# Attention with masks on VectorE, copied first keys and queries, and two heads in the halves of the rows; another order of the down products

## The reference

```python
# attention (x normalized first; B=8, S=512, D=256, 16 heads of 16)
scores = einsum('bhqd,bhkd->bhqk', Q, K) * 16 ** -0.5
scores = scores + where((abs(i - j) <= 64) | (i == 0) | (j == 0), 0, -inf)
x = x + (softmax(scores) @ V) @ Wo + bo
# experts: 16, each takes its 512 best of 4096 rows
topk_weight, topk_idx = top_k(softmax(flat_x @ gate_w.T, -1).T, 512)
g, u = xg @ Wg[e].T, xg @ Wu[e].T                # width 1024
eo = (gelu(g) * u) @ Wd[e].T * topk_weight       # the down product
out = scatter_add(eo) + shared_expert(x)
```

## Time and profile before

| | |
|---|---|
| median of three runs | 1411.79 us |
| the profiled execution, its own time | 1400.23 us |
| its span, first to last instruction | 1398.5 us |
| busy in the span: PE, PEld, DVE, ACT, POOL | 90%, 76%, 61%, 43%, 42% |
| mean granted TensorE clock | 0.952 of full |
| `qs<-qk_parts`, `ks<-qk_parts` | 96 transfers each, 128 KB |
| `qs<-mt` | 128 transfers, 4 KB |
| `rd<-rden` | 16 transfers, 256 KB |

### The profile page before, as it was taken

How to read it: one execution, slowest core, us unless ns; L and a number is a source line. 1 busy time by engine, 2 the same in 40 slices (tenths; PEclk the granted TensorE clock), 3 DMA queues, 4 the chain that set the end, 5 groups by cost and what they waited for, 6 DMA issues and landing times. The chain is left out here.

```text
span 1398.5 us, 26404 instructions
## 1 busy us (share of the span) xinstructions
PE 1256.7 (90%) x9930; PEld 1066.7 (76%) x9930; DVE 849.4 (61%) x1510; ACT 597.1 (43%) x1023; POOL 584.9 (42%) x530
## 2 busy tenths in 40 slices
PE   2995999999999972699999599999999999999997
PEld 2884777777777752588887578888888888888886
DVE  7874555555555512695688676666666666666641
ACT  1340544444444442354222255455455454545442
POOL 6000333332333342462200146666666666665554
PEclk9996999999999985699999789999999999999999
DMA  2778555555555416441003144434444433344411
GB/s 84 262 249 136 79 88 90 86 86 92 93 93 93 71 50 198 144 149 57 15 31 121 51 161 121 115 105 113 120 121 121 121 111 105 109 114 121 121 31 15
DMA packets 71284, 148.44 MB, mean 106 GB/s; under 512 B 14736, under 2 KB 31520, under 8 KB 64928
## 3 DMA queue, kind: packets, MB, share of 16 engines
q1 hardware_dynamic: 58544, 128.39, 35.4%
q0 software_dynamic: 12656, 18.90, 7.4%
HBM read 104.53 MB, written 42.21 MB: 105 GB/s over the span
## 5 line engine op out<-in xcount | busy, mean ns | idle before, releaser
L610 ACT ACTIVATE pt<-ps_p 128x512 f32<-128x512 f32 (+1 forms) x320 | 170.0, 582 | 218.1 <-PE ps_x L673 122.7
L550 DVE TENSOR_REDUCE mx<-ps_s 128x2 f32<-128x384 f32 (+2 forms) x160 | 143.9, 900 | 171.9 <-PE ps_x L651 154.9
L1803 POOL TENSOR_TENSOR h_lo<-h,h_hi 128x512 fp32r<-128x512 f32 x128 | 175.5, 1383 | 136.1 <-ACT h_hi L1839 135.8
L454 POOL TENSOR_SCALAR_AFFINE_SELECT pt<-pt 128x512 f32<-128x512 f32 x192 | 110.1, 597 | 273.4 <-ACT pt L610 273.4
L1913 PE MATMUL ps_gu<-xt_hi,w_hi 128*128 128x512 f32 x512 | 203.5, 397 | 2.1 <-DVE xt_lo L1862 2.1
L1913 PE MATMUL ps_gu<-xt_lo,w_hi 128*128 128x512 f32 x512 | 200.8, 392 | 0.0
L1913 PE MATMUL ps_gu<-xt_hi,w_lo 128*128 128x512 f32 x512 | 200.3, 391 | 0.0
L1878 DVE TENSOR_TENSOR h<-ge,ps_gu 128x512 f32<-128x512 f32 x128 | 87.8, 686 | 180.1 <-ACT ge L1833 167.9
L1740 DVE TENSOR_TENSOR w_lo<-w,w_hi 128x768 fp32r<-128x768 f32 x128 | 173.5, 1360 | 31.3 <-ACT w_hi L1735 27.8
L648 PE MATMUL ps_s<-ks,qs 96*128 96x256 f32 (+2 forms) x512 | 171.6, 398 | 0.0
L1812 POOL DMA_INDIRECT out<-ys,idx x64 | 131.1, 2049 | 73.3 <-ACT ys L1849 61.8
(11 more groups left out here) (221 smaller groups left out, 2891.9 us busy)
## 6 DMA issues: line engine op xcount, KB each, us to landing
w<-in_We SPq DMA_DIRECT2D x48, 1024.0 KB, 4.9
qk_parts<-qk SPq DMA_DIRECT2D x8, 2048.0 KB, 7.7
qs<-qk_parts SPq DMA_DIRECT2D x96, 128.0 KB, 3.6
ks<-qk_parts SPq DMA_DIRECT2D x96, 128.0 KB, 5.0
x<-in_x SPq DMA_DIRECT2D x16, 512.0 KB, 8.7
attn_t<-on SPq DMA_DIRECT2D x32, 256.0 KB, 3.7
ot<-attn_t SPq DMA_DIRECT2D x32, 128.0 KB
rd<-rden SPq DMA_DIRECT2D x16, 256.0 KB
```

Source lines behind the costliest of these rows:

```text
L454: last = pool.affine_select(out=part, in_=part, pattern=[[0, HQ], [sign, hi - lo]], compare_op=ALU.is_ge, fill=0.0, base=0, channel_multip ...
L550: last = dve.tensor_reduce(mxu[:, h:h + n, j], tile[:, :, 0:N0 if j == 0 else W[j]], AX, ALU.max)
L610: act.activation(pt[i][:, t % 2, h:h + nh], ps_p[:, n % 2].rearrange("p (h q) -> p h q", h=nh)[:, :, 0:W[i]], ACT.Exp, scale=SCALE).then_i ...
L1803: pool.tensor_tensor(h_lo[:, m], h32[:, (e * KI + m) % HB], h_hi[:, m].bitcast(F32), ALU.subtract).then_inc(hlo_s, 1)
```

## The change

Attention. The scratch tensor, `qs` and `ks` get rows of 516 (`ZS`): behind each tile of 128 stands a copy of column 0, which GpSimd makes in `project` before the store. A band of keys or queries then takes two more columns (`WZ`: 258, 258, 194) and contains key 0 or query 0 once or twice, so the two-column products, the separate maximum and the separate exponentials of query 0 are gone. The four heads of a unit stand two by two in the halves of the partitions: heads 0 and 2 in rows 0 to 49, heads 1 and 3 in rows 64 to 113. A product has 48 or 64 rows where it had 96 or 128. The loads become 12 per unit, the copies of the maxima 12 (two halves of four blocks and two single columns). The mask products of the maxima are gone: one VectorE instruction per head and tile (16 per unit) adds the mask to the scores and takes the maximum. `ps_s` becomes a ring of three banks, each with one head and tile. ScalarE does 8 exponentials per unit, each of two heads, where it did 10. GpSimd's selects are cut into pieces of 64 columns, 11 per unit. All loops over units are unrolled. SP's order per unit stays.

Experts. Row tiles 0 and 1 of the down product first take k tiles 0 to 6, then k tile 7 each; row tiles 2 and 3 follow as before.

```diff
-M_ROW = 96
+M_ROW = 48
+RING = 3
+ZC = P + 1
+ZS = NT * ZC
+WZ = [w + 2 for w in W]
+SIDE = ZC + 1
...
-        ks = att.enter_context(nc.sbuf_tensor("ks", [P, UB, HQ, S], F32R))
-        qs = att.enter_context(nc.sbuf_tensor("qs", [P, UB, HQ, S], F32R))
+        ks = att.enter_context(nc.sbuf_tensor("ks", [P, UB, HQ // 2, ZS], F32R))
+        qs = att.enter_context(nc.sbuf_tensor("qs", [P, UB, HQ // 2, ZS], F32R))
...
+                for b in range(B):
+                    pool.wait_ge(qlo_s, b * 4 + 4)
+                    rows = qk[:, b % 2].rearrange("p c m k i -> p (c m) k i")
+                    pool.tensor_copy(rows[:, :, :, P], rows[:, :, 0, 0:1].to_broadcast([P, 4 * KD, NT])).then_inc(z_s, 1)
...
-        ps_s = ctx.enter_context(nc.psum_tensor("ps_s", [P, 2, 2 * S], F32))
-        ps_p = ctx.enter_context(nc.psum_tensor("ps_p", [P, 2, S], F32))
-        ps_x = ctx.enter_context(nc.psum_tensor("ps_x", [P, 2, HQ, NT - 1, 2], F32))
-        key0, query0 = ps_x[:, 0], ps_x[:, 1]
+        ps_s = ctx.enter_context(nc.psum_tensor("ps_s", [P, RING, S], F32))
+        ps_p = ctx.enter_context(nc.psum_tensor("ps_p", [P, 2, 2, S], F32))
...
+                def near_only(u, i):
+                    pool.wait_ge(exp_s, u * SJ + 2 * (i + 1))
+                    for n in range(W[i] // WIN):
+                        first, sign = (n * (WIN + 1), 1) if n < 2 else (UPPER[i] + (n - 2) * (WIN + 1), -1)
+                        part = pt[i][:, u % 2, :, first:first + WIN]
+                        last = pool.affine_select(out=part, in_=part, pattern=[[0, HQ], [sign, WIN]], compare_op=ALU.is_ge,
+                                                  fill=0.0, base=sign * (n % 2) * WIN, channel_multiplier=-sign)
...
+                def load(u):
+                    b, t = u // UB, u % UB
+                    for dst, parts in ((qs, (0, 0, 1)), (ks, (2, 3, 2))):
+                        for n, part in enumerate(parts):
+                            heads = d["qk"][b, part, t * HQ * DH:(t + 1) * HQ * DH, :].rearrange(
+                                "(p r c) q -> r c p q", r=2, c=DH)
+                            for r in range(2):
+                                row = 64 * r + DH * n
+                                sp.dma_start(dst[row:row + DH, t].bitcast(F32), heads[r]).then_inc(qk_in[t], 16)
+
+                def m_rows(u):
+                    t = u % UB
+                    sp.wait_ge(mt_s, u + 1)
+                    for r in range(2):
+                        rows = qs[64 * r + M_ROW:64 * r + M_ROW + 2, t].bitcast(F32)
+                        for k in range(MK):
+                            dst = rows.rearrange("c p (j i) -> c (p j) i", j=NT)[:, :, 32 * k:32 * k + 32]
+                            sp.dma_start(dst, mt[32 * k + 16 * r:32 * k + 16 * r + 16, u % 2]).then_inc(m_in[t], 16)
+                        for z in (1, 2):
+                            sp.dma_start(rows[:, :, ZC * z + P:ZC * (z + 1)], mt[16 * r:16 * r + 16:NT, u % 2, 0:1],
+                                         allow_slow_non_contiguous=True).then_inc(m_in[t], 16)
...
+                m_rows(0)
+                for u in range(NU):
+                    b, t = u // UB, u % UB
+                    if u + 1 < NU:
+                        m_rows(u + 1)
+                    if u + UB < NU:
+                        sp.wait_ge(st_s, (u + 1) * SJ)
+                        load(u + UB)
+                    if u >= 1:
+                        store(u - 1)
...
+                    for g, (j, h) in enumerate(SCORES):
+                        dve.wait_ge(sc_s, u * SG + g + 1)
+                        n, m = (S, mask[:, 0:S]) if j == 0 else (WZ[j], mask[:, S:S + WZ[j]])
+                        dve.tensor_tensor_reduce(junk[:, (u * SG + g) % RING, 0:n], ps_s[:, (u * SG + g) % RING, 0:n], m, 1.0, -3e38, ALU.add, ALU.max,
+                                                 mx[:, u % 2, h % 2, h // 2, j:j + 1]).then_inc(mx_s, 1)
...
+                    if n >= RING:
+                        pe.wait_ge(mx_s, n + 1 - RING)
+                    rows = slice(64 * (h % 2), 64 * (h % 2) + M_ROW)
+                    q = tile_of(qs[rows, t, h // 2], j)
+                    k = ks[rows, t, h // 2]
+                    k = whole(k) if j == 0 else window(k, j)
+                    out = ps_s[:, n % RING]
+                    out = out.rearrange("p (k c) -> p k c", c=P) if j == 0 else out[:, 0:WZ[j]]
+                    pe.matmul(out, q, k, start=True, stop=True).then_inc(sc_s, 1)
...
+                AV = {3: 0, 5: 1, 6: 2, 7: 3}
+                for u in range(NU):
+                    for n in range(SJ):
+                        if u + 2 < NU:
+                            score(u + 2, 2 * n)
+                            score(u + 2, 2 * n + 1)
+                        exponents(u, n)
+                        if u >= 1 and n in AV:
+                            times_v(u - 1, AV[n])
...
+                    if e > 0:
+                        pe.wait_ge(ys_s, e * CT)
+                    contract(0, range(KI - 1))
+                    contract(1, range(KI - 1))
+                    contract(0, range(KI - 1, KI)).then_inc(y_s, 1)
+                    contract(1, range(KI - 1, KI)).then_inc(y_s, 1)
+                    for t in range(2, CT):
+                        pe.wait_ge(ys_s, e * CT + (t - 1))
+                        contract(t, range(KI)).then_inc(y_s, 1)
```

More of the change, by code:

```diff
@@ L176, in project @@
         qlo_s = sem("p_qlo")
+        z_s = sem("p_z")
         v_s = sem("p_v")
@@ L430, in attend, with whole, window, tile_of @@
         rden_out = sem("a_rden_out")
[L433 to L436, removed]
+        SCORES = [(j, h) for j in range(NT) for h in range(HQ)]
+        TJOBS = [(i, p) for i in range(NT) for p in range(HQ // 2)]
+        SG, SJ = len(SCORES), len(TJOBS)
         N0 = P + WIN
         MK = P // 32
-        def after(b, t, n):
-            return b + (t + n) // UB, (t + n) % UB
+        LOADS, MROWS = 12, 2 * MK + 4
+        def whole(tile):
+            return tile.rearrange("p (k c) -> p k c", c=ZC)[:, :, 0:P]
+        def window(tile, n):
+            return tile[:, ZC * n - WIN - 1:ZC * n - WIN - 1 + WZ[n]]
+        def tile_of(tile, n):
+            return tile[:, ZC * n:ZC * n + P]
         with nc.Block() as block:
@@ L466, in _ @@
                 pool.wait_ge(ones_s, 1)
-                for t in range(UB):
-                    take_v(0, t, t < 2)
+                for u in range(NU):
+                    take_v(u)
                     for i in range(1, NT):
[L470 to L475, removed]
+                        near_only(u, i)
@@ L572, in reciprocals @@
                     dve.reciprocal(den[:], den[:]).then_inc(rden_s, 1)
-                for t in range(UB):
-                    maxima(0, t, t < 2)
-                maxima(1, 0, False)
-                with dve.Fori(1, B - 1) as b:
-                    for t in range(UB):
-                        maxima(*after(b, t, 1), False)
-                        if t == 3:
-                            reciprocals(b - 1)
-                for t in range(1, UB):
-                    maxima(B - 1, t, False)
+                for u in range(NU):
+                    maxima(u)
+                    if u >= 9 and u % UB == 1:
+                        reciprocals((u - 9) // UB)
                 reciprocals(B - 2)
@@ L655, in st_job @@
[L655 to L665 removed]
+                        pe.wait_ge(qk_in[t], (b + 1) * 16 * LOADS)
@@ new lines, in exponents @@
+                def exponents(u, n):
+                    b, t = u // UB, u % UB
+                    i, p = TJOBS[n]
+                    if n == 0:
+                        pe.wait_ge(m_in[t], (b + 1) * 16 * MROWS)
+                    if u * SJ + n >= 2:
+                        pe.wait_ge(exp_s, u * SJ + n - 1)
+                    if i == 0:
+                        for r in range(2):
+                            pe.matmul(ps_p[:, n % 2, r, 0:N0], ident16[:], mask[:, 0:N0], start=True, stop=False,
+                                      skip_group_check=True)
+                    for r in range(2):
+                        rows = slice(64 * r, 64 * r + 64)
+                        k = tile_of(ks[rows, t, p], i)
+                        q, out = qs[rows, t, p], ps_p[:, n % 2, r]
@@ L675, in st_job, with near @@
                     last.then_inc(st_s, 1)
-                def times_v(b, t, i, first):
+                def near(rows, v, p, i):
+                    out = ps_o[rows, LO[i]:HI[i]]
+                    if i < NT - 1:
+                        pe.matmul(out.rearrange("p (k c) -> p k c", c=WIN), v,
+                                  p.rearrange("p (k c) -> p k c", c=WIN + 1)[:, :, 0:WIN],
+                                  start=False, stop=True, skip_group_check=True)
+                    else:
+                        pe.matmul(out[:, 0:WIN], v, p[:, 0:WIN], start=False, stop=True, skip_group_check=True)
```

(1 more changed line is left out.)

315 lines of the change are left out of this document (106 added, 209 removed).

## The result

The changed kernel takes 1466.87 us (median of 4 runs, 1464.81 to 1467.33) against 1409.43 us for the kernel before (4 runs, 1404.83 to 1412.71): ratio 1.041, 95% interval 1.037 to 1.044. It is slower, as forecast, but by 57 us where the forecast had 105 over its median. Its profiled execution took 1467.31 us with a span of 1465.6 and a mean granted clock of 0.794; before it was 1400.23, 1398.5 and 0.952. The difference between the two profiled executions is 67 us. Ratios go by the fast executions of a kernel, those within 1.5% of its fastest; only in the last experiment does this leave any out, three of seven.

The account below looks back on a forecast made before the run. TensorE sets attention's pace now; after the change SP's queue was to bind at 15.7 us a unit. 1400.2 + 115 (attention) - 10 (down products) = 1505, times 1.008 makes 1517 us; range 1410 to 1565.

Parts of the forecast that it names:

- SP becomes the bound: Attention: SP's issues take 15.7 us a unit, against the 12.1 a unit takes now, and set the period; chance 0.65.
- `den` and `rden` with their waits: Attention, SP's queue once in four units: 1.0 us for `den` and 3.9 for `rden`, 1.2 a unit.
- the attention's length: Attention from first loads at about 110.7 to TensorE's end near 631 us, not 516: +115 us.
- Loads begin at about 110.7: Start of attention: first loads at about 110.7 us, 110.4 now, with 0.3 for a new small GpSimd copy.
- Down products -10: Experts: the 1.07 us stop goes, a new one of 0.4 to 0.5 comes; net 0.6 x 16 = -10 us.
- The scale: Whole kernel: profiled forecast of 1505 us times 1.008, median of runs over profiled execution, makes 1517.
- TensorE's L = 10 at full clock, 16 at most: Attention: TensorE's pass through a unit, L, takes 10 us, between 8.3 and 16, the double at half clock.
- the third rival: Attention: TensorE's idle time lowers its clock, L up to 16, period 17.3, +43 us: 1560; chance 0.15.
- the 12.7 that the forecast called hidden: Attention: TensorE's pass L up to 12.7 us stays hidden behind SP's 15.7 a unit.
- The rule of A(u) + 3 + L: Attention: exponents begin about 3 us after SP issued unit u's copies, A(u); SP needs them done by A(u) + 15.7.
- Rival 2: Attention: SP doesn't bind, TensorE and VectorE set 9.5 to 10 us a unit; median 1328, faster; chance 0.10.
- VectorE: Attention: 16 fused add-and-maximum plus negating and transposing take 7.9 us a unit, bounds 6.65 to 9.

Follow-up runs that it names:

- the last experiment: Changed kernel with one head per product on whole rows, fills of `qs`/`ks` delayed, wait for `rden` store moved ahead of next `den` load: 1329.89 us against 1402.39, ratio 0.946.
- the kernel with extra copies: Kernel before, each of SP's four copies of the maxima followed by three more to scratch memory: 1488.86 us, ratio 1.063.
- rows alone: Kernel before with maxima in rows 48 and 49, exponents over 64 rows, one head per product, `ks` filled in one go: 1896.05 us, ratio 1.349.
- burst: Changed kernel with `ks` loads issued by ScalarE and single columns by GpSimd, plus 60 products of 128 rows before the first exponents: 1442.07 us, ratio 1.026.
- whole rows: Changed kernel without the halves: one head per product, scores 96 rows, exponents 128, 6 loads and 6 copies, fills delayed: 1350.28 us against 1401.35, ratio 0.965.
- with SP relieved: Changed kernel, nothing left out, loads of `ks` issued by ScalarE and single-column copies by GpSimd: 1435.96 us, ratio 1.025.

## Why the prediction was right or wrong

- **SP becomes the bound: right.** The copies' issues were forecast at 0.68 start to start and took 0.65 (7.84 us for twelve, forecast 8.1), the loads took 5.61 us (5.6). Twelve in a row, SP without waits for the exponents, PE released by the copies: all seen as the prediction asked; only the attention's end, near 597 and not near 630, was not. Two terms were too large: store and gaps 0.47 us for 0.8, and `den` and `rden` with their waits (59.18 - 4 x 13.92)/4 = 0.88 for 1.2 a unit; from the `rden` store to the next copies were 1.97 and 2.58 us here (301.66 to 303.63, 360.23 to 362.81) and not 3.9. In sum 14.80 for 15.7 us. From the copies of unit 3 to those of unit 29 the forecast had 406 us and the trace has 388.6 (163.4 to 552.0), which is most of the 21 us by which the attention's length, forecast at 631 - 110.7 = 520, came out shorter (499).
- **The projection, "that the change leaves alone": wrong, 14 us.** The step "Loads begin at about 110.7" read the change's effect on GpSimd at one place only, the small copy ahead of the store (0.3 us), and passed over the halved fills and the dropped third one. VectorE's 15.05 us row lay right beside them in the trace of before. The fills were that delay, as the kernel shows in which they wait: 1.38 us for the same row.
- **Down products -10: right.** -9.6 alone. The new stop was 0.2 us instead of 0.4 to 0.5.
- **The scale.** Another 12 of the 50 us come from multiplying by 1.008; the changed kernel's median and its profiled execution were the same. With 14.5 + 21 + 2 (behind the attention) + 12 the whole of 1517 - 1467 is accounted for.
- **TensorE's L = 10 at full clock, 16 at most: the mechanism missed, its price small.** The clock was at the lower level, as the third rival had it, but not because of idle time (the kernel with extra copies), rather with products of 48 and 64 rows (rows alone, burst, whole rows). The prediction let that rival fall if the halves run side by side. They do, in part: two exponent products of 512 columns take 0.59 us in the row below, where at half clock two of the earlier trace rows, one behind the other, would be 0.92. L was then 13.49 and not 12, 0.8 above the 12.7 that the forecast called hidden, and 1.7 above what the same rule gives at SP's real 14.80 (11.8). The period stayed SP's all the same, as the near absence of SP waits shows; the rival's 17.3 did not come. The rule of A(u) + 3 + L was too strict: in the trace the first mask product starts 1.0 us after the copies' last issue (311.42 to 312.42), and the last exponents' product ends at 324.27, 12.9 us after that issue, because value products and the next scores stand outside. SP needed it at 325.39. That this margin of 1.1 us was there is luck as far as the forecast goes.

```profile
312.85 0.79 PE L639 MATMUL ps_p<-qs,ks 64*128 64x512 f32 x2
313.44 0.63 PE L620 MATMUL ps_s<-ks,qs 48*128 48x512 f32 x2
```

- **And L = 10 itself** fitted the clock that it assumed: 9.94 us a unit with whole rows at 1.00. The sum of the products was 8.3; the 1.7 on top were a guess that fitted.
- **Rival 2 (SP does not bind, faster): wrong in two ways.** SP binds; and with SP relieved the kernel is still 2.5% slower than before, not 6% faster.
- **VectorE** was forecast at 7.9 us; its fused instruction follows itself after 0.61, 0.35 and 0.29 us (512, 258, 194 elements), so 4 x 0.61 + 8 x 0.35 + 4 x 0.29 + 0.7 = 7.1. It never bound.

A slip without weight: the prediction has 515.5 for the start of the last product with `vx`, and the earlier trace rows says 515.7.

What stays open: which property of the products the clock follows. The runs vary the rows and nothing finer, no kernel was run with 96 rows alone, and the last one falls from the upper level with 96 and 128.

## What to carry to other kernels

Count what a change adds to the queue that issues the transfers as carefully as what it takes from an engine: 24 issues, 13.5 us a unit, held up a TensorE that had fewer products than before. Before products are packed into halves of the rows, put one such stretch on the chip and read its granted clock: here the packing ran two products side by side and lost more through the clock than it won (13.49 us a unit for 9.94), while the same change without it was 3.5% faster than before. A wait for a store to land, in the middle of a queue, should stand where its result is needed and not behind the store; here that was worth 20 us more between medians, in a kernel whose executions spread by 56 us.

## What was not expected of the hardware

- Products over 48 and 64 rows ran at a granted clock of 0.50 even with TensorE busy 30.00 of 30 us, and a clock raised by whole-row products fell within one unit of them. Whole rows lost it too, in the last kernel, while PE was busy 6.00 of 6 us. The Trainium skill (TensorE: Matmul & The Clock Gate, "What's actually happening") ties the clock to how busy the engine has been; by busy time alone these stretches would be at the upper level.
- A mask product of 128 rows between products of 48 costs some 0.3 us more at half clock than twice what the pair took at full clock with 96 rows.
- GpSimd's fills held VectorE's normalisation, 15.05 us for four instructions that take 1.4; its statistics were not held.
- The same 4 KB from `mt` hold SP for 0.63 us when they go to two rows of `qs`, and three copies to contiguous memory take 1.33, 0.44 each (the kernel with SP's queue alone).
